# Two clamped sums written interleaved with a step of two, and read with that step by ScalarE's exponential

## What is computed

```python
li = x @ rel_W[:, :d].T
lj = x @ rel_W[:, d:].T
logits = li[:, :, None, :] + lj[:, None, :, :] + rel_b
relation_probs = jax.nn.softmax(logits, axis=-1)          # 3 classes for each pair (i, j)
bias = jnp.einsum('bijk,hk->bhij', relation_probs, logical_bias)
attn_scores = attn_scores + gate * bias
attn_weights = jax.nn.softmax(attn_scores, axis=-1)
```

## Time and profile before

| | |
|---|---|
| median of 3 runs | 4546.25 us (4544.65 to 4565.15) |
| profiled execution: time, span | 4540.25 us, 4538.5 us |
| VectorE busy | 3815.9 us, 84% |
| PE busy, ScalarE busy, GpSimd busy | 3592.7, 3321.6, 2042.4 us |
| clamps (L708) | 1024, 774.1 us, mean 758 ns |
| their exponentials (L668) | 512, 541.7 us, mean 1058 ns |
| mean granted clock of TensorE | 0.944 |

### The profile page before, as it was taken

One profiled execution on the slowest core, in us unless ns is written; L12 is line 12 of the kernel. 1 busy time (PEld: TensorE's weight loads), 2 busy tenths in 40 slices (PEclk: granted clock), 3 DMA queues, 4 the chain that ended last, 5 costly groups with the idle time before them and its releaser, 6 DMA issues. The chain is left out here.

```text
span 4538.5 us, 243862 instructions
## 1 busy us (share of the span) xinstructions
PE 3592.7 (79%) x106896; PEld 2680.9 (59%) x106896; DVE 3815.9 (84%) x6310; ACT 3321.6 (73%) x3946; POOL 2042.4 (45%) x1816
## 2 busy tenths in 40 slices
PE   7548888888888888888888888888888866399991
PEld 4306666666566666656666666666666655277771
DVE  4299999999899999999999999999999814277773
ACT  2008888988898898988898989999999961144440
POOL 0014445554454555544454555555555531533335
PEclk8659999999999999999999999999999996699996
DMA  5312222222222222222222222222222244344433
GB/s 105 73 38 68 67 68 68 71 70 66 65 70 67 67 69 70 66 67 68 66 70 67 71 69 68 68 70 66 75 64 70 67 120 140 121 151 147 154 127 120
DMA packets 368338, 371.66 MB, mean 82 GB/s; under 512 B 108416, under 2 KB 342272, under 8 KB 363296
## 3 DMA queue, kind: packets, MB, share of 16 engines
q1 hardware_dynamic: 358080, 338.08, 27.3%
q0 software_dynamic: 6144, 16.79, 1.2%
q10 hardware_dynamic: 3040, 0.98, 0.1%
HBM read 99.58 MB, written 46.40 MB: 32 GB/s over the span
## 5 line engine op out<-in xcount | busy, mean ns | idle before, releaser
L716 DVE TENSOR_REDUCE b_mxp<-b_mx 128x1 f32<-128x512 f32 x4096 | 2572.8, 679 | 126.5 <-PE b_mx L832 102.2
L690 ACT ACTIVATE b_pr<-b_sc 128x1024 f32<-128x1024 f32 x2048 | 1982.0, 1020 | 418.5 <-PE b_sc L813 399.8
L855 PE MATMUL b_acc<-b_pr,vp 128*32 128x128 f32 x32768 | 1141.4, 276 | 29.5 <-issue 27.1
L832 PE MATMUL b_mx<-kst,b_qt 64*128 64x512 f16 x4096 | 818.9, 393 | 413.1 <-DVE b_mxp L716 397.1
L855 PEld LDWEIGHTS b_acc<-b_pr,vp 128*32 128x32 f32 x32768 | 845.6, 110 | 287.4 <-issue 281.7
L613 POOL TENSOR_TENSOR b_ex<-b_ex 128x512 f32<-128x512 f32 x512 | 679.3, 1327 | 604.8 <-ACT b_ex L668 599.4
L801 PE MATMUL b_sc<-b_cm,b_rst 64*128 64x64 f16 x32768 | 765.8, 191 | 169.4 <-ACT b_pr L690 90.4
L801 PEld LDWEIGHTS b_sc<-b_cm,b_rst 64*128 64x128 f16 x32768 | 657.6, 95 | 338.1 <-ACT b_pr L690 147.0
L708 DVE TENSOR_SCALAR b_dl<-b_dj,b_const 128x512 f32<-128x512 f32 x1024 | 774.1, 758 | 67.9 <-ACT b_ex L668 39.2
L623 POOL CAST b_rhi<-b_ex 128x512 f16<-128x512 f32 x512 | 320.5, 626 | 1064.6 <-ACT b_ex L677 761.0
L813 PE MATMUL b_sc<-b_qt,kst 64*128 64x64 f16 x32768 | 686.4, 191 | 45.7 <-issue 42.0
(11 more groups left out here) (144 smaller groups left out, 1753.0 us busy)
## 6 DMA issues: line engine op xcount, KB each, us to landing
b_rst<-b_rhi SPq DMA_DIRECT2D x1024, 128.0 KB
b_rst<-b_rlo SPq DMA_DIRECT2D x512, 128.0 KB
c_w1r<-in_L_ffn_W_dram SPq DMA_DIRECT2D x23, 1024.0 KB, 4.9
c_w2r<-in_L_ffn_W_dram SPq DMA_DIRECT2D x23, 1024.0 KB, 4.9
expert_tokens<-c_zeros SPq DMA_DIRECT2D x23, 512.0 KB, 6.6
c_xb<-expert_tokens SPq DMA_DIRECT2D x23, 512.0 KB
expert_results<-c_y SPq DMA_DIRECT2D x23, 512.0 KB, 2.8
b_qt<-q_parts SPq DMA_DIRECT2D x64, 128.0 KB
```

The source lines that it names most:

```text
L690: nc.scalar.activation(pr[:, jt % 2, half, :], sc[:, half].rearrange("p a b -> p (a b)"), ACT.Exp).then_inc(s["p_ready"], 1)
L716: nc.vector.tensor_reduce(mxp[:, head, part:part + 1], mx[:, (bank + ab) % MX_RING, :], AX.X, ALU.max).then_inc(s["mx_used"], 1)
L832: pe.matmul(mx[:, (bank + ab) % MX_RING, :], qt[rows, slot4, pair, :], kst[rows, pair, j0:j0 + 512], start=True, stop=True).then_inc(s["mx ...
L855: ins = pe.matmul(acc[32 * (h % 4):32 * (h % 4) + 32, h // 4, :], vp[:, jt, VW * h:VW * h + 32], pr[:, jt % 2, h % 2].rearrange("p (a h i) ...
```

## The change

The buffer `dl` gets the index n of the two sums as its innermost one: the sums of one key lie side by side, as n = 0, n = 1. So each clamp writes 512 elements with a step of two elements (8 bytes), and the exponential reads two rows of 512 elements with that step, and writes `ex` contiguous as before. The buffer's size, the values, the number of instructions and all semaphores are as before.

```diff
-        dl = sb("dl", [P, 2, 2, JU])
+        dl = sb("dl", [P, 2, JU, 2])
...
-            nc.scalar.activation(ex[:, k].rearrange("p n j -> p (n j)"), dl[:, k].rearrange("p n j -> p (n j)"),
+            nc.scalar.activation(ex[:, k], dl[:, k].rearrange("p j n -> p n j"),
                                  ACT.Exp).then_inc(s["e_ready"], 1)
...
-            nc.vector.tensor_scalar(dl[:, side, n], dj[:, u, n], const[:, par, side, n:n + 1], EXP_MAX, ALU.add,
+            nc.vector.tensor_scalar(dl[:, side, :, n], dj[:, u, n], const[:, par, side, n:n + 1], EXP_MAX, ALU.add,
                                     ALU.min).then_inc(s["d_ready"], 1)
```

## The result

The changed kernel takes 4528.34 us (median of 9 runs, 4510.34 to 4542.69); the kernel before, run beside it, 4555.77 us (9 runs). The ratio is 0.9944, with a 95% interval of 0.9925 to 0.9962: faster by 0.56%, just past the 0.5% that I had set as the bound of "no change". The profiled execution has a span of 4532.5 us, 6.0 us under that of before; single executions differ by more than the effect, so the times come from the runs, and the profile only says how they arise.

The account below looks back on a forecast made before the run. VectorE was taken to bound the kernel, ScalarE second. Write, read and waits summed as 0 + 0 + 0 on the profiled 4540.25 us, 6 us under the runs' median; forecast 4546 us, within 15, range 4515 to 4750.

Parts of the forecast that it names:

- What bounds the kernel: Attention loop: VectorE leads at 95% busy, ScalarE second; clamps standing still behind GpSimd's sum cost VectorE 287 us.
- nearly a nanosecond: Attention loop's key step: each nanosecond added to a clamp adds nearly a nanosecond to the step.
- (a): VectorE's clamp: writing with a step of two was taken to cost 0 ns.
- 112 and 192 of the bounds: Clamp's stepped write: possible extra ns per clamp, from variance reads (115 us in all) and a step-of-8 subtraction (197 us).
- rival 3: Clamp: falls to one element at a time (739 ns), no longer excludes GpSimd; faster, 4527 to 4381 us; chance 0.10.
- The two rules: Clamp's write: two hits per 16-byte line means 0 cost; runs of two adjacent words means 168 ns, 172 us in all.
- (b): ScalarE's exponential over the clamped sums: reading with a step of two was taken to cost 0 ns.
- upper bound: Exponential's stepped read: at most 768 ns more, so 1058 becomes 1826 ns.
- Rival 2: Exponential's stepped read costs 768 ns more, ScalarE becomes the bound: 200 us, 4746; chance 0.12, including both read and write paying.
- The cover: ScalarE's 305.6 us idle ahead of its score exponentials in the loop, taken to hide a smaller cost of the read.
- Rival 4: Clamp against GpSimd's sum: only timing shifts, averaging out to a few us, inside 15; chance 0.57 shared with no cost.
- the case without a cost: Whole kernel: stepped write and read cost nothing, timing shifts included; 4531 to 4561 us, chance 0.57.

Follow-up runs that it names:

- short sum: Kernel before, with GpSimd's sum over 16 of its 512 elements, the rest left out: ratio 0.9722, 4425.3 us.
- write-only run: Changed kernel with the clamp's write still stepped by two but the exponential reading contiguously: ratio 0.9998 (0.9984 to 1.0013).

## Why the prediction was right or wrong

- *What bounds the kernel: right.* VectorE led, its clamps lost 280 ns each behind GpSimd, and ScalarE had room. The short sum shows what that is worth: 125 us for 264 us of clamp time, not the 287 of the sum of durations, since the others come next. So the prediction's "nearly a nanosecond" of step for each nanosecond of clamp was about twice too much in that direction.
- *(a) The clamp's write, taken as 0: right to a few ns.* Its median rose by 9 ns (14 in the write-only run), far under the 112 and 192 of the bounds, and the write alone changed no time that could be measured. The clamp kept its pace of two elements (487 ns and not 739), so rival 3's mechanism, the fall to one at a time, didn't occur.
- *The two rules weighed there.* By Measured stream behaviour on trn2 in the Trainium skill's Vector Engine (DVE) Microarchitecture Reference the clamp would have risen by an estimated 168 ns; it rose by 9. The measurement sides with the two hits per line of the Trainium skill's SBUF — State Buffer (section SBUF: two separate sides). That rule isn't exact either: the step cost the clamp 9 to 14 ns, and ScalarE's read 86.
- *(b) The exponential's read, taken as 0: 86 ns,* 0.084 ns per element, a ninth of the upper bound. Rival 2 needed 380 ns to decide. The cover hid it: ScalarE's groups have 42 us more of it in the loop (562.4 against 520.6), its idle time 25 us less, and the kernel didn't get longer.
- *Rival 4, timing shifts, is the step that failed,* by its size. I put it at a few us, because over 1024 clamps shifts should average out. They don't: the gaps between the starts of clamp and sum aren't spread evenly, 116 of 500 stood within 20 ns of each other, and a later sum moves this cluster as one. The shift of 86 ns left 228 clamps under a sum in place of 288. The gain was 27 us, against "inside my 15". I had the blocking, its price of 0.8 us a time and a row of a sum first by 0.29 us (2005.03 against 2005.32 in the earlier trace rows) before me, and costed a slower ScalarE only as a loss that is hidden or not. A list of the gaps would have shown the cluster. It would not have given the gain: taken turn by turn, 86 ns turn none of those 116, and make their clamps wait longer.
- *The other side.* The case that came, faster by a longer instruction, stood in none of the rivals with a price of its own; my chance of 0.09 for faster was given for another mechanism. The sign came from where I had looked, but not from what I had said. That 4528.34 lies in the range is in part luck: it is below the 4531 to 4561 that I gave the case without a cost, and the range went down to 4515 for rival 3, which didn't occur. The chances for faster and same, 0.09 and 0.58, are also off by 0.01 from their parts (0.10 less 0.02, and 0.57 with 0.02), which changes nothing.

What stays open: what puts so many sums of the kernel before at 120 to 140 ns ahead of a clamp, how a delay of 86 ns, less than that lead, comes to spare 60 clamps, and how much the step costs by itself once no collision is left (the intervals overlap).

## What to carry to other kernels

Where two engines exclude each other for whole instructions, and the bounding one often comes second by a little, look at the gaps between their starts before costing any edit. Where many gaps stand close to zero, a delay of some ns doesn't average out. What it is worth, and in which direction, the list alone doesn't say; here a delay put on purpose on the engine with idle time showed it. Then order the two on purpose (one wait on the engine with idle time, or another place for the instruction); here this gave 2 to 2.6%, about four times what the step gave by accident. And when a change that only makes an instruction longer makes a kernel faster, lengthen the same instruction in another way before believing in the change.

## What the runs showed of the hardware that I had not expected

- A 4-byte read with a step of two costs ScalarE 86 ns over 1024 elements (1058 to 1144, the single ones from 1104 to 1173, where the contiguous ones keep to 1039 to 1062), while a write with that step costs VectorE 9 to 14 ns over 512. A step of two isn't quite free on either.
- On ScalarE a bias from memory costs 91 ns (1149), and a scale from memory on top another 91 (1240), with a bias of zero and a scale of one.
- The order in which they start decides between VectorE's clamp and GpSimd's instructions: first by 0.21 us, the sum cost the clamp 0.88 us; second by 0.28 us, it cost it nothing, and itself took 1.33 in place of 1.28. Closer behind it costs the sum more: 1.54 at 50 to 100 ns (median of 20 in the trace of before), 1.59 at most. The clamp's longest is 1.62 in place of 0.48.
